# Down projection beside the score pass in half tiles, its row sums folded into the products, and one more output projection tile moved there

## The reference, cut to what matters

```python
xn = layer_norm(x)                                   # x: 8 x 512 x 512
q, k, v = rope(xn @ Wq.T), rope(xn @ Wk.T), xn @ Wv.T  # 16 heads of 32
s = (softmax(causal(q @ k.T / sqrt(32))) @ v) @ Wo.T

def bitlinear(x, w):                                 # w ternary: sign * mean(abs(w))
    return einsum(layer_norm(x) , w_ternary)         # forward: quantised layer norm
h = gelu(bitlinear(xn, w_fc))                        # 512 -> 2048
g = silu(bitlinear(h, w_proj))                       # 2048 -> 512
out = x + s * g
```

## Time and profile before

| what | value |
|---|---|
| median of 3 runs | 1173.84 us (1173.41 to 1173.95) |
| the profiled execution: its own time, its span | 1173.02 us, 1171.3 us |
| PE busy | 1138.3 us (97%) in 7580 matmuls |
| DVE, ACT, POOL busy | 842.5, 792.0, 522.0 us |
| chain that ended last, by engine | PE 83%, DVE 7%, ACT 6% |
| granted clock of TensorE | 0.999 |
| one batch (from 462.01 to 601.08 us) | 139.07 us |

### The profile page before, as it was taken

How to read it: one execution, slowest core, us unless ns; L and a number is a source line. 1 busy time by engine, 2 the same in 40 slices (tenths; PEclk the granted TensorE clock), 3 DMA queues, 4 the chain that set the end, 5 groups by cost and what they waited for, 6 DMA issues and landing times.

```text
span 1171.3 us, 20065 instructions
## 1 busy us (share of the span) xinstructions
PE 1138.3 (97%) x7580; PEld 562.5 (48%) x7580; DVE 842.5 (72%) x1442; ACT 792.0 (68%) x1492; POOL 522.0 (45%) x908
## 2 busy tenths in 40 slices
PE   4989999999999999999999999999999999999997
PEld 3555545445444554445544454444544455444553
DVE  7987947797458975588546984579745897558854
ACT  4787974488825878269763797448882587826964
POOL 2135442563526625275243644256352662527434
PEclk9999999999999999999999999999999999999999
DMA  8490001920019001450007401091011900045011
GB/s 305 153 126 21 2 29 37 123 76 1 30 26 155 20 3 28 54 126 19 31 1 82 98 20 30 1 124 75 2 30 26 154 20 3 27 57 88 19 39 37
DMA packets 52586, 67.31 MB, mean 57 GB/s; under 512 B 9352, under 2 KB 34312, under 8 KB 51976
## 3 DMA queue, kind: packets, MB, share of 16 engines
q1 hardware_dynamic: 52488, 66.02, 28.6%
HBM read 31.98 MB, written 8.40 MB: 34 GB/s over the span
## 4 chain that ended last, share of the span: by engine, by line
PE 83%; DVE 7%; ACT 6%; DMA 1%; issue 1%; SPq 1%; POOL 0%; DVEq 0%; ACTq 0%
PE banks L405 22%; PE banks L531 18%; PE banks L562 18%; PE banks L649 5%; PE banks L510 5%; PE banks L618 5%; ACT arena L848 4%; PE banks L421 2%; PE banks L517 2%; DVE mix L1081 2%; PE banks L435 1%; ACT banks L826 1%; DVE arena L1014 1%; DMA stacks<-split_buf 1%; PE banks L442 1%
## 5 line engine op out<-in xcount | busy, mean ns | idle before, releaser
L562 PE MATMUL banks<-projT,arena 128*128 128x512 f16 x1024 | 286.2, 377 | 0.0
L826 ACT ACTIVATE banks<-banks,mix,scl 128x512 f32<-128x512 f32 (+2 forms) x384 | 248.6, 657 | 13.9 <-POOL mix L1301 10.9
L1081 DVE TENSOR_REDUCE mix<-banks 128x1 f32<-128x384 f32 (+3 forms) x352 | 215.1, 634 | 31.0 <-PE banks L517 19.6
L531 PE MATMUL banks<-xT,fcT 128*128 128x512 f16 x1024 | 227.2, 379 | 0.1
L848 ACT ACTIVATE arena<-banks,scl 128x1280 f32<-128x1280 f32 x128 | 164.7, 1328 | 65.7 <-PE banks L618 62.4
L1284 POOL TENSOR_TENSOR split_buf<-xr_buf,split_buf 128x512 f16<-128x512 f32 x64 | 74.0, 1178 | 247.2 <-ACT split_buf L772 247.2
L1293 POOL TENSOR_TENSOR xh_buf<-xh_buf 128x512 f32<-128x512 f32 x120 | 152.2, 1269 | 58.4 <-ACT xh_buf L795 55.1
L405 PE MATMUL banks<-xT,qkT 128*128 128x512 f16 x768 | 168.7, 379 | 0.0
L531 PEld LDWEIGHTS banks<-xT,fcT 128*128 128x128 f16 x1024 | 98.6, 98 | 118.7 <-ACT xh_buf L795 3.7
L1301 POOL TENSOR_SCALAR mix<-mix,scl 128x1 f32<-128x1 f32 (+1 forms) x288 | 76.1, 265 | 152.6 <-DVE mix L1081 143.0
L800 ACT ACTIVATE banks<-banks,scl 128x512 f32<-128x512 f32 x128 | 84.8, 663 | 84.3 <-PE banks L531 84.0
(11 more groups left out here) (153 smaller groups left out, 1566.5 us busy)
## 6 DMA issues: line engine op xcount, KB each, us to landing
stacks<-split_buf SPq DMA_DIRECT2D x192, 128.0 KB, 5.1
out_dram<-arena SPq DMA_DIRECT2D x32, 256.0 KB, 2.3
xr_buf<-in_L_attn_x_dram SPq DMA_DIRECT2D x7, 1024.0 KB, 7.3
resid<-in_L_attn_x_dram SPq DMA_DIRECT2D x28, 256.0 KB, 5.0
stacks<-in_L_ffn_w_fc_dram SPq DMA_DIRECT2D x1, 4096.0 KB, 25.9
arena<-in_L_ffn_w_proj_dram SPq DMA_DIRECT2D x1, 4096.0 KB, 14.6
mix<-norm_row SPq DMA_DIRECT2D x8, 256.0 KB, 3.8
xr_buf<-in_L_attn_x_dram SPq DMA_DIRECT2D x4, 256.0 KB, 3.5
```

The source lines that it names most:

```text
L531: mm = pe.matmul(banks[:, UP_BANKS[f % NUB], :], fcT[:, c, f * P:(f + 1) * P], xT[:, part, c, :], start=(c == 0 and part == 0), stop=(c == ...
L562: mm = pe.matmul(banks[:, 6 + t % 2, :], lhs, projT[:, f, :], **ends)
L826: mm = nc.scalar.activation(block, block, ACT.Exp, scale=col(EXP_SCALE), bias=exp_bias[:, i, h0 + k:h0 + k + 1], accum_out=row_sum[:, i, h ...
L1081: nc.vector.tensor_reduce(row_max[:, i, h0:h0 + n], scores_of(r), AX_X, ALU.max).then_inc(max_ready, 1)
```

## The change

- `down()` works in half tiles: halves h = 0..5 (t = h // 2) into the banks 7, 5, 6 in turn. The ternary weights get a column of ones at each side (`proj_ones`, 514 columns), so that one half of a tile has 257 columns with the row sum among them, and the other 256. A step is one chunk f of a half: two matmuls (high and low part) of 257 or 256 columns. The 128x1 matmuls of L561 go; those of L593 (tile 3) stay. Tile 3 stays whole, in bank 7.
- ACT copies four halves (tiles 0 and 1) to `gate_sum`, of which `gate` is now a view that starts at column 1. Tile 2 stays in PSUM in two halves; DVE takes its mean out (`centre`) right behind `neg_mean`. The sums are read in two instructions in place of one.
- `OUT_EARLY` is 1 in place of 2: output tile 1 moves from the dense stage to the score pass; late tiles 1 to 3 are scaled behind rounds 4, 7 and 12 and get x added behind rounds 6, 7, 9, 10, 14 and 15. Before, late tiles 2 and 3 were scaled behind rounds 4 and 7.
- `split_rotated(3)` stands behind the GELU of f = 2 (f = 0 in the first batch).
- Score round 2 stands behind the first four companions; before, it came ahead of them. Its bank is 0 in place of 5.
- All token statistics stand on DVE between `split_parts` of the maxima and the copy of the transposed maxima. POOL's normalise steps stand behind the last bias: six ahead of the `rstd` power, the rest behind it. SP writes the norms behind the maxima's DMA.
- In the second pass head 0 takes banks 0 to 2 and head 1 banks 3 to 5 (before the other way round); head 1 waits for the first `centre` in place of the sums.

```diff
-S_BANKS = (3, 4, 5, 2, 1)
+S_BANKS = (3, 4, 0, 2, 1)
-OUT_EARLY = 2
+OUT_EARLY = 1
-STATS_AFTER = {9: 0, 11: 1}
-LATE_STATS_AFTER = {5: 2, 7: 3}
-NORM_FROM = 16
+LN_EARLY = 6
+DOWN_BANKS = (7, 5, 6)
+N_HALF = 2 * (NT - 1)
+DW = D + 2
-FIRST_LEAD = (0, 0, 11, 13, 16)
-LEAD = (0, 0, 11, 17, 20)
+FIRST_LEAD = (0, 2, 11, 13, 16)
+LEAD = (0, 4, 11, 17, 20)
...
-        projT = sb("projT", [P, FC, D], F16)
+        proj_ones = sb("proj_ones", [P, FC, DW], F16)
+        projT = proj_ones[:, :, 1:D + 1]
...
-                if not last:
-                    store_norms(b + 1)
                 sp.wait_ge(maxT_ready, b + 1)
                 sp.dma_start(q_stack[KS:KM, :, :], maxT[:, :]).then_inc(max_dma, 16)
                 if not last:
+                    store_norms(b + 1)
                     spread_norms(b + 1)
...
-                    if f >= FC - EARLY:
+                    if FC - EARLY <= f < FC - 1:
                         score_round(f - (FC - EARLY))
...
                 def down():
-                    for t in range(NT):
-                        if t < 2 and not first:
-                            pe.wait_ge(scaled_ready, b * NT - 1 + t)
...
+                    for h in range(N_HALF):
+                        t, low = h // 2, h % 2
+                        cols = slice(low * (D // 2 + 1), D // 2 + 1 + low * D // 2)
+                        if t == NT - 2:
+                            cols = slice(1 + low * D // 2, (D // 2 + 1) + low * (D // 2 + 1))
...
+                        if h >= 3:
+                            pe.wait_ge(down_kept, b * 4 + h - 2)
+                        for f in range(FC):
...
-                            if t < NT - 1:
-                                pe.matmul(banks[:, 0, t:t + 1], lhs, ones16[:, 0:1], **ends)
-                            mm = pe.matmul(banks[:, 6 + t % 2, :], lhs, projT[:, f, :], **ends)
+                            for part in range(2):
+                                mm = pe.matmul(banks[:, DOWN_BANKS[h % 3], 0:cols.stop - cols.start],
+                                               hid[:, part, f, t * P:(t + 1) * P], proj_ones[:, f, cols],
+                                               start=(f == 0 and part == 0), stop=(f == FC - 1 and part == 1))
...
                 for r in range(NR):
-                    if r >= EARLY:
+                    if r >= EARLY - 1:
                         score_round(r)
...
                     if h == 1:
-                        pe.wait_ge(sums_read, b + 1)
+                        pe.wait_ge(centred, b * NT + 1)
...
-                    if f == 0:
+                    if f == (0 if first else 2):
                         split_rotated(3)
                     if f >= 1:
                         square(f - 1)
...
                 split_parts(max_parts, row_max[:], -1.0, max_step, b * 3, max_split)
+                if not last:
+                    statistics(b + 1)
...
+                dve.wait_ge(down_ps, b * (N_HALF + 1) + N_HALF)
+                halves = banks[:, 5:7, 0:D // 2]
+                nc.vector.scalar_tensor_tensor(gate[:, 2, :].rearrange("p (a c) -> p a c", a=2), ...
...
+                for _ in range(0 if last else LN_EARLY):
+                    next(steps)
                 pool.wait_ge(var_ready, b + 1)
                 nc.gpsimd.tensor_tensor(ffn[:, 8, :], ffn[:, 5, :], minus_half[:], ALU.pow).then_inc(rstd_ready, 1)
+                for _ in steps if not last else ():
+                    pass
```

More of the change, by code:

```diff
@@ L396, in ternary_row_sums @@
                 for f in range(FC):
-                    mm = pe.matmul(banks[:, 7, :], ones16[:], projT[:, f, :], start=(f == 0), stop=(f == FC - 1))
+                    mm = pe.matmul(banks[:, 6, :], ones16[:], projT[:, f, :], start=(f == 0), stop=(f == FC - 1))
                 mm.then_inc(rowsum_ps, 1)
@@ L460, in body @@
                         pe.wait_ge(w_kept, ND)
-                    if t == 1 and first:
-                        pe.wait_ge(attn_scl_step, 4)
                     if t >= 2:
@@ L564, in down @@
+                    pe.wait_ge(down_kept, b * 4 + 4)
+                    for part in range(2):
+                        for f in range(FC):
+                            mm = pe.matmul(banks[:, 7, :], hid[:, part, f, S - P:S], projT[:, f, :],
+                                           start=(f == 0 and part == 0), stop=(f == FC - 1 and part == 1))
+                            if f == FC - 1 and part == 1:
                                 mm.then_inc(down_ps, 1)
@@ L592, in body @@
                     for part in range(2):
-                        pe.matmul(banks[:, 0, NT - 1:NT], hid[:, part, f, S - P:S], ones16[:, 0:1],
+                        pe.matmul(banks[:, 6, D // 2 + 1:D // 2 + 2], hid[:, part, f, S - P:S], ones16[:, 0:1],
                                   start=(f == 0 and part == 0), stop=(f == FC - 1 and part == 1))
@@ L596, in body @@
                 for t in range(NT):
-                    mm = pe.matmul(banks[:, 0, NT + t:NT + t + 1], sq_sum[:, t * P:(t + 1) * P], ones32[:], start=True, stop=True)
+                    mm = pe.matmul(banks[:, 6, D // 2 + 2 + t:D // 2 + 3 + t], sq_sum[:, t * P:(t + 1) * P], ones32[:], start=True, stop=True)
                 mm.then_inc(sq_ps, 1)
@@ L810, in body @@
                     act.wait_ge(rowsum_ps, 1)
[L811 removed]
+                    nc.scalar.copy(w_rowsum[:], banks[:, 6, :]).then_inc(rowsum_kept, 1)
                 for r, (i, h0, n) in enumerate(ROUNDS):
@@ L1108, in body @@
                         round_weights(u)
-                    if f in STATS_AFTER and not last:
-                        token_statistics(b + 1, STATS_AFTER[f])
                     if f >= FC - EARLY:
@@ L1213, in _ @@
             nc.gpsimd.memset(mask_q[:], 0.0)
+            for edge in (0, D + 1):
+                nc.gpsimd.memset(proj_ones[:, :, edge:edge + 1], 1.0)
             nc.gpsimd.memset(selector[:], 0.0)
@@ L1286, in body @@
                 if not first:
-                    for t in range(2):
+                    for t in range(OUT_EARLY):
                         add_x(b - 1, t)
@@ L1293, in body @@
                     nc.gpsimd.tensor_tensor(sq_sum[:], sq_sum[:], squares[f % NSQ], ALU.add).then_inc(sq_added, 1)
-                steps = normalise_steps(b + 1)
                 for r in LONG[BIAS_DVE:]:
                     i, h0, n = ROUNDS[r]
-                    if r >= NORM_FROM and not last:
-                        next(steps, None)
                     pool.wait_ge(max_ready, b * NR + r + 1)
```

115 lines of the change are left out of this document (58 added, 57 removed).

## The result

The changed kernel takes 1162.74 us (median of 4 runs, 1162.43 to 1163.22) against 1173.87 (1173.41 to 1173.95) for the kernel before in the same session: the ratio is 0.9907, with a 95% interval of 0.9892 to 0.9923. It is faster by 0.9%. The forecast was 1165.0 in a range of 1157 to 1173. The profiled execution took 1162.8 us around a span of 1161.0, where the one before took 1173.02 around 1171.3.

What follows compares the result with a forecast made beforehand. Bound taken: PE's time up to head 0, plus an unchanged second pass set by ACT's exponentials. Seven batches at -1.2 (-8.5) and the first at -0.2 take 1173.02 to 1164.3; median 0.8 above gives 1165.0, range 1157 to 1173.

Steps and rivals of the forecast that it cites:

- the named case: Whole kernel: the forecast outcome, a time of 1162 to 1169 us, chance 0.55.
- Term 1: Down projection on PE: 96 half-tile steps of 0.2204 us replace pairs of 0.2412, a gain of 2.0 us a batch.
- Term 2: Output tile moved from dense stage to score pass: 2.6 us moves, nothing on PE, and ACT gets slack.
- Term 3: Up stage: copies behind the third GELU delay a square, so PE stands 0.93 us ahead of chunk 4.
- Term 4: DVE statistics behind the maxima fit with 0.6 us slack, cost nothing; 0.15 us of PE idle time is gained.
- Term 5: POOL's steps, SP's order, late x tile, score round 2 and exchanged banks: nothing that is waited for moves.
- The first batch: ACT and DVE set the pace there; only PE's last steps before the transposes get shorter: -0.2 us.
- A (no stall): Up stage: the stall at chunk 4 isn't there; gain 15 us in seven batches, 1158.5 us, chance 0.17.
- B (odd start): Down projection: loads or odd weight starts slow PE; from 7.5 ns each the gain goes; 1180 or 1194, chance 0.12.
- C: Late x tile, statistics or ACT in the rounds takes back about 1.2 us a batch: 1173.5 us, chance 0.13.

Runs made afterwards that it cites:

- experiment 3: Changed kernel with OUT_EARLY at 2 again, so the output tile is back in the dense stage: 1172.6 us, ratio 0.9987 to the kernel before.
- experiment 9: Changed kernel with the down projection's weights moved by one element, making 96 fewer starts odd: 1160.71 us, ratio 0.9889 to the kernel before.
- experiment 10: Changed kernel with the last rope pair's copies one behind GELU 1 and one behind GELU 2, ahead of the squares: 1158.25 us.
- experiment 1: Changed kernel with the last rope pair's copies back behind the first GELU in every batch: 1162.99 us, ratio 0.9906 to the kernel before.
- experiment 7: Changed kernel with tile, copies, statistics and POOL's steps put back, leaving half tiles, and SP storing norms ahead of the maxima's DMA: 1170.05 us.
- experiments 6: Changed kernel with tile, copies, statistics and POOL's steps put back, leaving half tiles, but norms still stored behind the maxima's DMA: 1188.34 us.
- Experiment 11: Changed kernel with copies split behind GELU 1 and 2, weights moved one element, and first batch's statistics back in its up stage and rounds: 1157.47 us.

## Why the prediction was right, and what was mis-sized

The sign, the range and the named case (1162 to 1169) were right. The sum was -1.2 us for a batch, measured -1.86. That the time fell into the named case is partly luck: batches 1 to 7 gave 12.2 us where I had summed 8.5, and the first batch (0.67 lost, not 0.2 won) and a start-up 1.18 longer hid some 2 us of that. Without those two the time would have been near 1160.7, inside the range but below the named case. Step by step:

- **Term 1** (half tiles, -2.0): right. A step is 0.2210 us and not 0.2204: 96 x (0.2412 - 0.2210) = 1.94. The ones' price of 0.025 was confirmed by putting them back (24.7 ns). Nor does each half carry that price on top of its columns: the halves were spaced at 0.1105.
- **Term 2** (the moved tile, 0 on PE): right as a sum, -2.59 and +2.60. Its reason, that it gives ACT slack, is right. How much it is worth was not worked out: with two tiles in the dense stage PE stands 0.95 us in the rounds (experiment 3), 0.94 when both stages are added (36.27 + 40.97 against 33.68 + 42.62).
- **Term 3** (copies behind GELU 2, +0.93): right in mechanism, measured +0.77. In the trace the loss is shared: about 0.24 us ahead of chunk 3, from DVE's late scaling, and the rest ahead of chunk 4. That DVE's delay doesn't add to the sum holds too: in batch 3 of experiment 9 all 0.83 us stand ahead of chunk 4, and the stage takes the same 25.01. Having the copies one by one gives back 0.52 of the 0.77; 0.25 stays (experiment 10). The reason given for the later place holds as well: beside the moved tile, early copies wait for a DMA (experiment 1).
- **Term 4** (statistics, 0 and a gain of 0.15): this is the term that was mis-sized. That they fit behind the maxima was right; the slack is 0.96 where I had 0.6. But I counted as a gain only a part of the 0.21 us of idle time that the windows of before showed. Those windows hide waits, since a matmul's modelled busy time runs into the next; start-to-start, one round alone began 0.36 us late. The trace of before had the whole size in its last batch, which has no statistics: 0.65 us less in the rounds. I also followed DVE alone, where the wait runs through POOL's bias and ACT's exponential to PE. Idle time gone from the rounds is 0.69, not 0.15. With the half tiles the same work costs more: 1.18 us (42.17 against 40.99 in the last batch of experiment 7). A likely reason is that PE then has less work of its own between the rounds; no run shows it apart.
- **Term 5** (the rest, 0): right for the middle batches. The late x tile, SP's order and the exchanged banks left no gap. SP's order has a risk that I had not seen: with norms that are ready early, it costs 4 us in some batches (experiments 6 and 7). The changed kernel is spared because POOL's steps behind the last bias make the norms ready late.
- **The first batch** (-0.2): wrong. The statistics there come on the chain: the way from the transposes to head 0 is 0.87 longer and the up stage 0.23, the rounds are only 0.50 shorter, and the batch lost 0.67. Experiment 11 gets 0.92 back.

By the terms as measured: -1.94 + 0.77 - 0.69 = -1.86.

How the parts hang together is best read from the stages of the versions, in this order: half tiles alone give 0.48 in the rounds (42.65 to 42.17, experiment 7). Statistics and POOL's steps out of the rounds give another 1.20 (to 40.97, experiment 3). The moved tile gives 0.94. The up stage takes 0.77 back. The sum is -1.85. In another order the shares differ: taken out first, the statistics and steps give 0.65 (the last batch of before). The gain of the half tiles is PE's, but before the other edits ACT, POOL and DVE could not follow, and PE spent three quarters of it waiting. The summary for the rivals: A (no stall) fell, the stall is there. B (odd start) is real at about 2 ns for a matmul of 512 columns and about 1 for a half, not 7.5. C did not come: the x tile and the statistics had the room I gave them.

What stays open: why the last semaphore update of the maxima's DMA comes late when the norms' DMAs and an instruction packet fall together, as they did in batches 1, 3 and 5; and where the differences of 1 to 2 us in the start-up come from.

## What to carry to other kernels

When two engines are level, a saving on one is worth what the others let through: measure it together with the edit that gives them room, and don't call either edit worthless because it does little alone. Count idle time from the starts of instructions, not from busy shares, before saying how much there is to gain. Look also for a pass in the trace that lacks the work in question, as the last batch lacks the statistics: it is an experiment that has already run. A small operation inserted in an engine's order is paid where its followers are waited for: follow it through every queue behind it (here ACT, POOL's sums, ACT's later square, PE), and prefer places where the next instruction waits for somebody else anyway.

## What the runs showed of the hardware

- A matmul of one column with its own weight load costs PE 24.7 ns in a stream of matmuls of 256 and 257 columns (2.30 us for 93), and 25 ns beside 512 columns (0.2412 against 0.2165 us).
- Halves of 257 and 256 columns, each with its load, are spaced at 0.1105 us, about 3.5 ns above their columns at 2.4 GHz (40 matmuls, 32 of them of 257 columns; the granted clock there is 1.00).
- A moving operand that starts at an odd 2-byte element costs little: 1.9 ns in a matmul of 512 columns (218.9 against 217.0), 0.5 to 1.1 ns in one of 256 or 257.
- Four DMAs of 0.5 KB, in over 500 packets of 4 B, issued right behind a 48 KB one on the same queue, went with a landing of the latter some 4 us late in three of seven batches, in two kernels: those in which a packet of instructions (queue 14, 8192 B) started in the same 4 us. The data packets were on time; the last semaphore update was not. With the same DMAs issued 20 us ahead, or 3.6 us behind, none was late.
- Where PE had stood 4.4 us at head 0, its granted clock was 0.50 (1.2 GHz) from 583.20 to 586.60, around its start at 583.68, and 1.00 (2.4 GHz) behind.
